# Layer 1's q and k as fp16 parts, scores in three fp16 products, low part of the probabilities on GpSimd

## The reference

```python
h = jnp.maximum(_layernorm(x, axis=-1), 0.0)
q = split_heads(h @ Wq)
k = split_heads(h @ Wk)
v = split_heads(h @ Wv)
sim = jnp.einsum('bhid,bhjd->bhij', q, k) * scale
sim = jnp.where(adjacency_mask[:, None, :, :], sim, neg)
attn = jax.nn.softmax(sim, axis=-1)
out = jnp.einsum('bhij,bhjd->bhid', attn, v)
x = x + out @ Wo + bo
```

## Time and profile before

| | |
|---|---|
| median of three runs | 2714.02 us |
| the profiled execution | 2716.61 us |
| its span, first to last instruction | 2714.8 us |
| mean granted clock of TensorE | 0.979 of full speed |
| PE / DVE / ACT / POOL busy in the span | 96% / 73% / 65% / 52% |

### The profile page before, as it was taken

How to read it: one execution, slowest core, us unless ns; L and a number is a source line. 1 busy time by engine, 2 the same in 40 slices (tenths; PEclk the granted TensorE clock), 3 DMA queues, 4 the chain that set the end, 5 groups by cost and what they waited for, 6 DMA issues and landing times. The chain is left out here.

```text
span 2714.8 us, 62488 instructions
## 1 busy us (share of the span) xinstructions
PE 2602.1 (96%) x20886; PEld 1398.9 (52%) x20886; DVE 1983.0 (73%) x6360; ACT 1753.7 (65%) x5019; POOL 1401.7 (52%) x2800
## 2 busy tenths in 40 slices
PE   6899999999999999999999999947999999999997
PEld 3355555555555555555555555533555555555554
DVE  4477778777877777777777777755777777777765
ACT  3366666666666666666666666645777777777774
POOL 1355455545555554555455555523656556555552
PEclk8999999999999999999999999968999999999999
DMA  4266766776666677657766766565777778777763
GB/s 138 51 131 138 153 128 134 149 142 131 137 151 144 134 142 149 132 134 148 145 137 133 153 143 131 114 171 105 165 165 161 165 163 172 167 157 167 158 148 93
DMA packets 944336, 385.33 MB, mean 142 GB/s; under 512 B 857488, under 2 KB 859024, under 8 KB 944016
## 3 DMA queue, kind: packets, MB, share of 16 engines
q1 hardware_dynamic: 944016, 381.34, 66.1%
HBM read 112.76 MB, written 67.11 MB: 66 GB/s over the span
## 5 line engine op out<-in xcount | busy, mean ns | idle before, releaser
L525 ACT ACTIVATE probs<-probs,negmax 128x128 f32<-128x128 f32 x1024 | 399.0, 392 | 468.3 <-DVE negmax L121 468.3
L437 POOL TENSOR_TENSOR o_sb<-o_sb,xres 128x512 f32<-128x512 f32 x128 | 162.8, 1272 | 502.2 <-DVE o_sb L664 497.5
L163 PE MATMUL ps_pj<-wm_hi,hT 128*128 128x512 f16 x1024 | 327.0, 381 | 22.7 <-DVE wm_lo L689 15.0
L163 PE MATMUL ps_pj<-wv_hi,hT 128*128 128x512 f16 x1024 | 326.7, 380 | 0.0
L163 PE MATMUL ps_pj<-hT,wk_hi 128*128 128x512 f16 x1024 | 305.8, 380 | 0.0
L163 PE MATMUL ps_pj<-hT,wq_hi 128*128 128x512 f16 x1024 | 304.5, 379 | 0.0
L1163 ACT ACTIVATE l_probs<-l_probs,l_negmax 128x128 f32<-128x128 f32 x512 | 199.4, 391 | 152.7 <-DVE l_negmax L121 152.7
L1099 POOL TENSOR_TENSOR l_h<-l_h 128x512 f16<-128x512 f32 x124 | 143.6, 1158 | 272.7 <-ACT l_h L1142 180.1
L121 DVE CUSTOM_DVE_ANT_0 probs<-ps_sc,mask 128x128 f32<-128x128 f32 x1024 | 235.6, 285 | 40.7 <-PE ps_sc L852 40.6
L646 DVE SCALAR_TENSOR_TENSOR c<-cprobs,c 128x512 f16<-128x512 f32 x256 | 182.4, 712 | 81.3 <-ACT c L532 81.0
L532 ACT ACTIVATE c<-cprobs 128x512 f16<-128x512 f32 x256 | 160.8, 628 | 119.3 <-DVE cprobs L640 115.9
(11 more groups left out here) (197 smaller groups left out, 6673.6 us busy)
## 6 DMA issues: line engine op xcount, KB each, us to landing
xg<-in_x SPq DMA_DIRECT2D x128, 256.0 KB, 3.2
xres<-in_x SPq DMA_DIRECT2D x128, 256.0 KB, 3.0
x_scratch<-o_sb SPq DMA_DIRECT2D x128, 256.0 KB, 2.4
out<-l_o_sb SPq DMA_DIRECT2D x128, 256.0 KB, 3.3
room<-x_scratch SPq DMA_DIRECT2D x124, 256.0 KB, 3.2
cpT<-c SPq DMA_TRANSPOSE x256, 3.2
mask_u<-in_adj SPq DMA_DIRECT2D x32, 64.0 KB, 2.4
hT<-h SPq DMA_TRANSPOSE x128, 3.3
```

Of the source, the lines that this page charges most:

```text
L163: last = pe.matmul(out, a(kt), b(kt), start=(n == 0), stop=(n == 3 * kts - 1))
L437: nc.gpsimd.tensor_tensor(o_sb[:, j % 2], o_sb[:, j % 2], xres[:, j % 2], ALU.add).then_inc(res_done, 1)
L525: last = nc.scalar.activation(probs[:, i], probs[:, i], ACT.Exp, bias=negmax[:, u % 2, i:i + 1], scale=-1.0, accum_out=zsum[:, u % 4, hh:h ...
```

## The change

q and k are no longer kept in fp32. ACT copies the high part out of PSUM in fp16 (qk_high), without the factor, and DVE subtracts it from the same PSUM bank to give the low part (qk_low). qk_low is DVE's first step in round n, ahead of add_residual(n-4). project_qk(i) now waits for qk_low(i-1), and the first scores of a group wait for qk_low of the group's last call. The scores are three fp16 products for each head where one fp32 product stood. Since q and k now come without their factors, the factor goes into the operation of the row maximum as a per-partition scalar (score_scale), and the mask's value for excluded pairs is scaled likewise (excluded).

The low part of the probabilities (p_low) goes from DVE to POOL, behind add_bias and ahead of the factors. nprobs gets a second buffer, and DVE's normalise waits for p_low two graphs back. The factor F16_SCALE goes from p_high and p_low into the reciprocal: DVE first multiplies zsum by 1/F16_SCALE.

```diff
-        q_sb = sb("q_sb", [P, 2, PAIRS1, QUAD * P])
-        k_sb = sb("k_sb", [P, 2, PAIRS1, QUAD * P])
+        qk_hi = {k: sb(f"{k}_hi", [P, 2, PAIRS1, QUAD * P], F16) for k in "qk"}
+        qk_lo = {k: sb(f"{k}_lo", [P, 2, PAIRS1, QUAD * P], F16) for k in "qk"}
...
-        nprobs = sb("nprobs", [P, HB, P])
+        nprobs = sb("nprobs", [P, 2, HB, P])
...
@@ POOL
+            def p_low(n):
+                pool.wait_ge(phi_done, count(n + 1))
+                nc.gpsimd.tensor_tensor(p16[:, n % 2, 1], nprobs[:, n % 2], p16[:, n % 2, 0], ALU.subtract).then_inc(plo_done, 1)
...
             for n in range(B):
                 if n + 9 < B:
                     h_low(n + 9)
                 if n >= 3:
                     add_bias(n - 3)
+                p_low(n)
                 if n % QUAD == 1 and n + 11 < B:
                     factors(n + 11)
...
@@ ACT
-                if c % 2 == 0:
-                    nc.scalar.activation(q_sb[:, g % 2, c // 2], ps_pj[0][:], ACT.Copy, scale=unscale["q"]).then_inc(q_done, 1)
-                else:
-                    nc.scalar.activation(k_sb[:, g % 2, c // 2], ps_pj[0][:], ACT.Copy, scale=unscale["k"]).then_inc(k_done, 1)
+                nc.scalar.copy(qk_hi["qk"[c % 2]][:, g % 2, c // 2], ps_pj[0][:]).then_inc(qkhi_done, 1)
...
-                nc.scalar.activation(p16[:, n % 2, 0], nprobs[:], ACT.Copy, scale=F16_SCALE).then_inc(phi_done, 1)
+                nc.scalar.activation(p16[:, n % 2, 0], nprobs[:, n % 2], ACT.Copy).then_inc(phi_done, 1)
...
@@ DVE
+            def qk_low(i):
+                g, c = divmod(i, QUAD)
+                kind = "qk"[c % 2]
+                dve.wait_ge(qkhi_done, count(i + 1))
+                nc.vector.tensor_tensor(qk_lo[kind][:, g % 2, c // 2], ps_pj[0][:], qk_hi[kind][:, g % 2, c // 2],
+                                        ALU.subtract).then_inc(qklo_done, 1)
...
-                nc.vector.reciprocal(rec[:], zsum[:, n % 2]).then_inc(rec_done, 1)
-                dve.wait_ge(rec_done, count(n + 1))
-                nc.vector.tensor_tensor(nprobs[:], probs[:], rec[:].unsqueeze(2).to_broadcast([P, HB, P]),
+                dve.wait_ge(plo_done, count(n - 1))
+                nc.vector.tensor_scalar(rec[:], zsum[:, n % 2], 1.0 / F16_SCALE, None, ALU.mult).then_inc(rec_done, 1)
+                dve.wait_ge(rec_done, count(2 * n + 1))
+                nc.vector.reciprocal(rec[:], rec[:]).then_inc(rec_done, 1)
+                dve.wait_ge(rec_done, count(2 * n + 2))
+                nc.vector.tensor_tensor(nprobs[:, n % 2], probs[:], rec[:].unsqueeze(2).to_broadcast([P, HB, P]),
                                         ALU.mult).then_inc(np_done, 1)
-
-            def p_low(n):
-                dve.wait_ge(phi_done, count(n + 1))
-                nc.vector.scalar_tensor_tensor(p16[:, n % 2, 1], nprobs[:], F16_SCALE, p16[:, n % 2, 0], ALU.mult,
-                                               ALU.subtract).then_inc(plo_done, 1)
...
             for n in range(B):
+                if n + QUAD < B:
+                    qk_low(n + QUAD)
                 if n >= 4:
                     add_residual(n - 4)
...
-                if n + 1 < B:
-                    p_low(n + 1)
...
@@ PE
-                if c % 2 == 0:
-                    pe.wait_ge(k_done, count(2 * g + c // 2))
-                else:
-                    pe.wait_ge(q_done, count(2 * g + c // 2 + 1))
+                pe.wait_ge(qklo_done, count(i))
...
                 for pr in range(PAIRS1):
-                    for b in range(2):
-                        rows = slice(DH * b, DH * b + DH)
-                        mm = nc.tensor.matmul(ps_s[:, b, pr * P:(pr + 1) * P], q_sb[rows, g % 2, pr, cols], k_sb[rows, g % 2, pr, cols],
-                                              start=True, stop=True)
+                    for i, (q_part, k_part) in enumerate(((qk_hi, qk_hi), (qk_hi, qk_lo), (qk_lo, qk_hi))):
+                        for b in range(2):
+                            rows = slice(DH * b, DH * b + DH)
+                            mm = nc.tensor.matmul(ps_s[:, b, pr * P:(pr + 1) * P], q_part["q"][rows, g % 2, pr, cols],
+                                                  k_part["k"][rows, g % 2, pr, cols], start=(i == 0), stop=(i == 2))
```

More of the change, by code:

```diff
@@ L114, in slot, with mask_scores @@
     return 2 * (hh % 2) + hh // 2
-def mask_scores(nc, dve, s_ready, n, masked, scores, mask, negmax):
+def mask_scores(nc, dve, s_ready, n, masked, scores, mask, negmax, scale):
     dve.wait_ge(s_ready, n)
     for i in range(HB):
-        last = nc.vector.tensor_tensor_reduce(masked[:, i], scores[:, i // 2, (i % 2) * P:(i % 2 + 1) * P], mask, -1.0,
+        last = nc.vector.tensor_tensor_reduce(masked[:, i], scores[:, i // 2, (i % 2) * P:(i % 2 + 1) * P], mask, scale,
                                               FLOAT_MAX, ALU.add, ALU.min, negmax[:, i:i + 1])
@@ L1108, in _ @@
             factors(QUAD)
+            pool.wait_ge(scale_chain, SCALE_OPS)
             convert_mask(0)
@@ L1185, in _ @@
                 nc.scalar.activation(w_hi[k][:], raw[k], ACT.Copy, scale=w_st[:, n, 2:3]).then_inc(prep_hi, 1)
-            act.wait_ge(scale_chain, SCALE_STEPS * len("qkvo") + 2)
             for c in range(QUAD):
-                qk_copy(c)
+                qk_high(c)
                 v_high(c)
@@ L1199, in _ @@
                 if n + QUAD < B:
-                    qk_copy(n + QUAD)
+                    qk_high(n + QUAD)
                 if n + 10 < B:
@@ L1285, in _ @@
             for j in range(QUAD):
+                qk_low(j)
                 v_low(j)
@@ L1289, in _ @@
             normalise(0)
-            p_low(0)
             for i in range(3 * QUAD, 15):
```

30 lines of the change are left out of this document (18 added, 12 removed).

## The result

The changed kernel takes 2803.28 us, the median of five runs (2800.8 to 2810.38), against 2714.02 for the kernel before (five runs, 2710.21 to 2717.51): a ratio of 1.0329, with an interval of 1.0314 to 1.0344. The direction is the one forecast, the size is not: +89 us where +36 was said, and the time lies outside the range of 2708 to 2778. The profiled execution took 2803.28 us, with a span of 2801.5 and a mean granted clock of 0.971.

A forecast was written before the change was run, and what follows sets the result against it. PE bounds the kernel at 6.51 us a graph; afterwards four graphs take 4 times 6.31 + 2.02 = 27.26 instead of 26.04, +38 over 31 blocks, +36 with the ends: 2752.6 us, median 2750, range 2708 to 2778.

The forecast's parts named there:

- PE's part: Score products on PE: twelve fp16 products take 0.43 us instead of 0.65, so PE needs 6.29 us a graph.
- The circle: Chain of waits over DVE and ACT, add_residual to add_residual: from 5.53 to 6.31 us a graph, level with PE.
- The scale in the row maximum ... nothing: Row maximum on DVE: a per-partition operand costs nothing; 0.1 us if each of four lasted a tenth longer.
- third rival: POOL's third wide operation collides with DVE's nprobs in every graph: 0.35 us each, period 7.16, 2793 us; 9%.
- one such meeting in four graphs: A POOL operation delaying DVE's nprobs, 0.35 us, once in four graphs: said to lie within the forecast's range.
- The scaling of zsum is one more small step before the reciprocal: 0.21: On DVE ahead of the reciprocal: the new small operation adds 0.21 us a graph.
- The stall of 2.02 once in four graphs: DVE's add_residual waits 2.02 us for a late store once in four graphs, making the average graph 6.81 us.
- The forecast's path: POOL's p_low, behind queued work, delays transpose_p and SP's store behind it: 15.82 us against 13.80 available.
- this wait comes from a late DVE and is in the circle: PE's wait for qk_low at a group's first graph: no cost beyond the circle's.
- rival four: PE's new stops lower its granted clock: 96 us more, 2846 us; 3%.
- What would have shown it: Profile signs: twelve products in 0.43 us, row maximum spacing 6.3 and once 8.3, one 2 us store wait a block.
- three signs of being wrong: In the middle: PE busy 99%, nprobs above 1.0 us on average, or granted clock under 0.95.

The follow-up runs named there:

- sf: Changed kernel with each round's store first on SP and F16_SCALE multiplied in by nprobs instead of the zsum scaling: 2701.75 us.
- best2: Changed kernel with stores first on SP, F16_SCALE in nprobs (no zsum scaling), and qk_low behind add_residual in three rounds of four: 2720.6 us.
- fold: Changed kernel without the small scaling of zsum, F16_SCALE multiplied in by nprobs: 2762.4 us.
- store: Changed kernel with each round's store issued first on SP, ahead of transpositions and load: 2752.6 us.
- qkold: Changed kernel with q, k and scores in fp32 as before; p_low on POOL and the zsum scaling kept: 2750.4 us.
- qsf: Changed kernel with q, k and scores in fp32 as before, stores first on SP, and F16_SCALE in nprobs instead of the zsum scaling: 2709.4 us.
- store3: Changed kernel with the store ahead of transpose_h and load_x, still behind transpose_p, in every fourth round of SP: 2772.8 us.
- fill: Changed kernel with ten 512-column products into a spare PSUM bank on PE, ahead of a group's first scores: 2793.7 us.
- late: Changed kernel with qk_low behind the row maximum on DVE in three rounds of four: 2793.1 us.
- swap: Changed kernel with qk_low between add_residual and the row maximum on DVE in three rounds of four: 2820.9 us.
- sfs: Changed kernel with stores first, F16_SCALE in nprobs, the constant -1.0 in the row maximum, and factors back in qk_high and qk_low: 2702.8 us.

## Why the prediction was right in direction and wrong in size

- **PE's part** held. The twelve products step by 0.44 us (0.43 said), and PE's own pace is 6.31 a graph in sf and best2 (6.29 said).
- **The circle** was close: 6.44 where 6.31 stood. By terms: the row maximum +0.24, which the step "The scale in the row maximum ... nothing" excluded with an allowance of 0.1; qk_high and its way to DVE 0.60 instead of 0.70, since the copy without a factor takes 571 ns, not the 683 of the copy before (the prediction gave ACT's lost scale no price either). The prediction's own rows had a hint: add_residual, with a per-partition factor, takes 0.75, p_low, with a constant, 0.69, and it read the difference as that of a PSUM input. qk_low reads PSUM without a factor and takes 0.69. That the circle would be level with PE was right. The net 0.13 is worth 16 us (times 124); the row maximum's part alone is 0.24, 30 us, and taking the constant back gave 31.
- **The step that failed most is the third rival's mechanism**, the meeting of POOL and nprobs, which the sum left out and the text allowed "one such meeting in four graphs", at 0.35. It happens once in four graphs, and it costs 1.5. The kernel before had such meetings nearly as often already: from 1950 to 2640 us nprobs took 0.84 to 1.06 in 22 of 106 graphs and 1.77 in one, while the circle of 5.53 was read from a graph without it, so even the 0.35 belonged in the sum. The cause of the rest is a term priced on its own: "The scaling of zsum is one more small step before the reciprocal: 0.21". That small step takes part in the meeting (0.83 instead of 0.17), and POOL's add_bias has started before nprobs does, so that nprobs waits for it as well. 1.5 times 31 is 46 us. Removing the small step gives 41 (fold), its own 0.21 in each graph included, and 51 where the store is out of the way (store to sf), of which 1.3 of 1.7 us a block lie in the graph of the meeting.
- **The sum of the third rival** was not by the prediction's own model either. There the store is late against two circles; with 0.35 more in each, the stall is 2.02 - 0.70 = 1.32, and the period 6.66 + 0.33 = 6.99 and not 7.16. Two small slips beside it move nothing: 2303.04 less 2301.93 is 1.11 (1.12 said), and 5.89 less 0.55 is 5.34 (the bound says 5.40).
- **The stall of 2.02 once in four graphs** has the right size, 8.4 for the fourth graph where the circle takes 6.44, and that is partly luck: only 1.1 us a block of it are waits for a store. Its path was only partly the one described. The forecast's path, p_low on POOL to transpose_p to the store, is real: in qkold moving the store gives back 21 of the 36 us, and the rest goes with the small scaling (qsf), so that these 36 equal the forecast's +36 by chance. In the changed kernel the chain shown comes from k_low over PE's scores and project_v to transpose_h and the store, and 30 us went when the store was put ahead of transpose_h but not of transpose_p (store3). The prediction saw this wait and closed it with "this wait comes from a late DVE and is in the circle". It isn't: while PE stands still, what follows from PE, the tile that transpose_h needs, is late too, and the store behind it.
- **The clock** (rival four) was right in kind and wrong in size. PE is busy 90%, with one stop a block, and in 12 of 24 blocks the granted clock over the 7 us behind the stop was 0.56 to 0.78 on average (0.76 in most); fill shows about 10 us in all, not 96. The rule that the prediction cited, from the Trainium skill ("TensorE: Matmul & The Clock Gate", HAM oscillation), that a wait in each round of a loop sets the clock back, holds here in half of the rounds: a stop of 3.02 us that ended at 1982.76 left it at 1.00, one of 2.99 us that ended at 2011.03 did not. Why in these and not in those is open.
- **What would have shown it**: row maximum to row maximum was to be 6.3 in three graphs of four and 8.3 in the fourth. It is 6.43, 6.44, 8.20 and 8.21. One of the two long ones is the meeting, which no step had. None of the three signs of being wrong came: PE is busy 90% and not 99%, the clock in the middle is 0.97, and nprobs is 0.90 us on average, under the 1.0 that was named, since the average hides the one graph in four with 1.52 behind three with 0.69.

Together: 6.81 was said for a graph, 7.32 measured in the middle. The circle gives +0.13, the meeting +0.35, the stalls and late starts +0.03 (0.53 for 0.505).

Open: how exactly the 51 us that go with the store's place divide between POOL's path and PE's in the changed kernel. store3 takes 30 of them with transpose_p still ahead of the store; but the two paths end in the same queue and hide each other, so the other 20 are no clean price of POOL's.

## What to carry to other kernels

When a change brings a second engine's chain level with the bound, price every small instruction on that chain, and ask of each whether it can meet another engine's wide operation: here one of four columns, 0.17 us alone, cost 41 us. Look at the longest times of an instruction and not at its average. When several paths end in one in-order queue (the store behind the transpositions), shortening one of them can show little (late gained 10 us, swap lost 18); look at the place where they end, since moving the store there was one edit worth 51 us. With that and without the small scaling the same change is 0.42% faster than the kernel before (2701.75 us) instead of 3.29% slower.

## What the runs showed of the hardware

- The row maximum's custom instruction over 128 columns takes 345 ns with a per-partition scalar from SBUF and 285 with a constant.
- The same step for qk_low over 512 columns: 751 ns with a per-partition factor (sfs), 692 without.
- A tensor_scalar of 128x4 on DVE waits out a wide two-input operation of POOL (0.83 us instead of 0.17); a reciprocal of the same size doesn't (0.18 in all graphs).
- In the changed kernel, behind such a wait POOL's next operation starts ahead of DVE's next two-input one, which then waits again (1.52 instead of 0.69) in 23 of 23 cases.
- A copy of 128x512 from PSUM on ACT takes 571 ns to fp16 without a factor, 687 to fp16 with a per-partition one (sfs) and 683 to fp32 with one (the kernel before).
